# A two-layer gated cross-attention block: the experts of a group issued between the two halves of the attention of the next groups

## What is computed

```python
# layer 0, attention: 16 heads of 16; the last 16 context tokens have weights and a softmax of their own
q = ln(heads(norm(x) @ Wq + bq))
k, v = ln(heads(ctx[:, :48] @ Wk + bk)), heads(ctx[:, :48] @ Wv + bv)
kd, vd = ln(heads(ctx[:, 48:] @ Wkv_dca + bkv_dca))      # v not normalised
x = x + tanh(g_xattn[0]) * ((attn(q, k, v) + attn(q, kd, vd)) @ Wo + bo)
# layer 0, feed-forward: 16 experts of width 64, the best 4 of each token, and one shared expert
w = topk(softmax(norm(x) @ gate_w.T), 4)
y = sum_e w[e] * (silu(h @ Wg[e]) * (h @ Wu[e])) @ Wd[e] + sigmoid(h @ sg) * shared(h)
x = x + tanh(g_ffn[0]) * y
# layer 1: attention with 16 heads of 128 (8 for keys and values), then a SwiGLU of width 688
```

## Time and profile before

| | us |
|---|---|
| median of three runs | 492.94 |
| profiled execution, its own time | 496.02 |
| its span, first to last instruction | 494.2 |
| TensorE matmul busy | 414.4 (84%) |
| VectorE busy | 342.6 (69%) |
| ScalarE busy | 206.3 (42%) |
| GpSimd busy | 161.9 (33%) |

### The profile page before, as it was taken

One profiled execution on the slowest core, in us unless ns is written; L12 is line 12 of the kernel. 1 busy time (PEld: TensorE's weight loads), 2 busy tenths in 40 slices (PEclk: granted clock), 3 DMA queues, 4 the chain that ended last, 5 costly groups with the idle time before them and its releaser, 6 DMA issues. The chain is left out here.

```text
span 494.2 us, 8704 instructions
## 1 busy us (share of the span) xinstructions
PE 414.4 (84%) x2996; PEld 389.1 (79%) x3004; DVE 342.6 (69%) x754; ACT 206.3 (42%) x405; POOL 161.9 (33%) x194
## 2 busy tenths in 40 slices
PE   0647794957666899999999899999999999879996
PEld 0536683847555898999999899999999999869995
DVE  4775749577520666858686398988988988966652
ACT  3264536535222133334334246455555546513331
POOL 3013322142230022222313144464464464334332
PEclk9958596885955699999999899999999999989999
DMA  8103001010110003020020100100100100000000
GB/s 248 43 1 96 32 8 57 0 65 0 28 79 1 0 1 106 0 90 16 19 87 0 58 12 2 55 1 0 55 0 0 44 1 1 1 0 23 23 17 27
DMA packets 6633, 16.03 MB, mean 32 GB/s; under 512 B 1090, under 2 KB 4291, under 8 KB 6100
## 3 DMA queue, kind: packets, MB, share of 16 engines
q1 hardware_dynamic: 6612, 15.75, 9.7%
HBM read 14.70 MB, written 1.05 MB: 32 GB/s over the span
## 5 line engine op out<-in xcount | busy, mean ns | idle before, releaser
L1421 POOL TENSOR_SCALAR work<-work,lut_step,lut 128x344 f32<-128x344 int32 (+1 forms) x60 | 41.7, 709 | 57.4 <-DVE work L1348 55.7
L291 PE MATMUL ps<-wB_hi,workr 128*128 128x256 f32 x224 | 52.0, 295 | 6.0 <-POOL workr L1576 4.6
L291 PE MATMUL ps<-xT_hi,wB_hi 128*128 128x256 f32 x176 | 52.5, 298 | 0.0
L291 PE MATMUL ps<-xT_lo,wB_hi 128*128 128x256 f32 x176 | 50.7, 288 | 0.0
L291 PE MATMUL ps<-xT_hi,wB_lo 128*128 128x256 f32 x176 | 50.7, 288 | 0.0
L291 PE MATMUL ps<-wN_hi,shared_r 128*128 128x256 f32 x256 | 47.8, 281 | 1.3 <-DVE x L1335 1.3
L1014 POOL TENSOR_TENSOR workr<-work,workr 128x256 fp32r<-128x256 f32 (+1 forms) x36 | 23.0, 638 | 69.7 <-ACT workr L897 69.7
L291 PEld LDWEIGHTS ps<-wB_hi,workr 128*128 128x128 f32 x224 | 38.9, 191 | 8.1 <-POOL wB_lo L1426 3.8
L1363 DVE COPY_PREDICATED work<-work 128x1376 f32<-128x1376 int32 (+5 forms) x36 | 42.5, 1182 | 2.7 <-DVE work L1363 0.3
L291 PEld LDWEIGHTS ps<-wN_hi,shared_r 128*128 128x128 f32 x256 | 40.3, 188 | 1.5 <-DVE shared_r L1325 1.5
L291 PE MATMUL ps<-xT_hi,wM_hi 128*128 128x256 f32 x128 | 37.5, 293 | 4.0 <-ACT work L1189 2.4
(11 more groups left out here) (199 smaller groups left out, 1188.9 us busy)
## 6 DMA issues: line engine op xcount, KB each, us to landing
stage<-in_wC SPq DMA_DIRECT2D x4, 1280.0 KB, 5.3
stage<-in_wB SPq DMA_DIRECT2D x4, 768.0 KB, 4.3
stage<-in_idx SPq DMA_DIRECT2D x4, 536.0 KB, 3.4
stage<-in_wA SPq DMA_DIRECT2D x2, 512.0 KB, 5.5
out<-x SPq DMA_DIRECT2D x4, 256.0 KB, 2.2
x<-in_x SPq DMA_DIRECT2D x1, 768.0 KB, 6.9
ctx_T<-in_ctx_T SPq DMA_DIRECT2D x1, 512.0 KB, 7.8
ctx_n<-in_ctx_n SPq DMA_DIRECT2D x4, 128.0 KB, 2.2
```

What stands on the lines that cost most here:

```text
L291: last = nc.tensor.matmul(out, l, r, start=start and i == 0, stop=stop and i == 2)
L1421: nc.gpsimd.tensor_scalar(lev[:, j, 0:n], bits[:, 0, 0:n], lut_step[:, j:j + 1], lut[:, 2 * j:2 * j + 1], ALU.mult, ALU.add).then_inc(*C[" ...
```

## The change

Stages A and B become one sequence of five steps, g = -1 to 3, written out instead of looped: step g holds the experts of group g, the second half of attention of group n = g + 1 and the first half of group m = g + 2, as far as they exist. Step -1 has no experts, step 2 no first half, step 3 the experts alone. C and D stay.

- The banks are dealt anew. B has two gate banks (0 and 1) where it had three, one bank (2) for logits, comb and spread, where spread had two, and one (3) for both tiles of the output. A has banks 4 to 7: the scores of tile 0 in 4 and 5, those of tile 1 in 6 and 7, and everything of the second half (turned probabilities, values, output) in 6 and 7. gate_up(k) waits for h2(k - 2), spread(k) for h3(k - 1), probabilities of tile 1 for the copy of tile 0's.
- All 16 joins move to step 3, two behind each gate_up, over four banks. The weights are loaded in turn into stage and into wC_odd, which lies where A's weights were, and so is loaded once A has ended.
- The four quarters of wB are loaded at the start, ahead of wS and sel on SP's queue, into wB_raw, which lies under wB_lo. They are split in step -1, and TensorE waits for the last of them ahead of step 0.
- Normalising x moves from VectorE to ScalarE, with an offset -mean * rstd made by two further instructions on GpSimd. The copies of the keys' pieces on VectorE (six of eight) move to ScalarE, in three lots: 0, then 1 and 2, then 3. A's turned x has tiles of its own (xTA).
- Where tiles are no longer free by the order of the lists, waits are added (vz for pv_done, ctxm for kv_done, xn for xT_done).

The diff, cut to this (unchanged indentation of eight columns left out):

```diff
+with nc.sbuf_tensor("as_loaded", [P, 2 * NWA + GROUPS * GB], F32) as loaded:
+    wC_odd, wB_raw = loaded[:, 0:GCW], loaded[:, 2 * NWA:2 * NWA + GROUPS * GB]
...
+def front_pool_offset(pool, f):
+    front_pool(pool, f)
+    pool.wait_ge(*front["rstd_ready"].at(f, 1))
+    pool.sem_inc(waited, 1)
+    for t in range(TILES):
+        nc.gpsimd.tensor_scalar(offset[:, t:t + 1], mv[:, t, 0:1], rstd[:, t:t + 1], -1.0, ALU.mult,
+                                ALU.mult).then_inc(*front["offset_ready"].up())
+def front_norm_act(act, f, g):
+    act.wait_ge(*front["offset_ready"].at(f, TILES))
+    if not isinstance(f, int) or f:
+        act.wait_ge(*front["xT_done"].at(f, 0))
+    for t in range(TILES):
+        nc.scalar.activation(xn[:, t, :], x[:, g * TILES + t, :], ACT.Identity, scale=rstd[:, t:t + 1],
+                             bias=offset[:, t:t + 1]).then_inc(*front["xn_ready"].up())
...
+SC = (4, 6)
+KV = (5, 4)
+QK = (4, 5)
+PROBS, VALUES = 6, 6
+A_FRONT, B_FRONT, TURN_OUT, OUT_A = 4, 1, 6, 7
...
+def pe_A_probs(pe, n, t):
+    pe.wait_ge(*A["probs_ready"].at(n, 2 * t + 2))
+    if t == 0:
+        pe.wait_ge(*A["exp_ready"].at(n, TILES))
+    else:
+        pe.wait_ge(*A["pT_ready"].at(n, t))
...
+def pe_A_values(pe, n, t):
+    if t == 0:
+        pe.wait_ge(*A["pT_ready"].at(n, TILES))
+        pe.wait_ge(*A["kv_ready"].at(n, 6))
...
+def act_A_k(act, n, pairs=range(PAIRS0)):
+    act.wait_ge(*A["qT_done"].at(n, 2))
+    for p in pairs:
+        for i, (lo, hi) in enumerate(PARTS):
+            r = slice(32 * p, 32 * p + 32)
+            nc.scalar.activation(kx[r, :, p, lo:hi],
+                                 ps[r, QK[1], :].rearrange("p (k n) -> p k n", n=S)[:, :, lo:hi], ACT.Identity,
+                                 scale=cols[r, 2 + 2 * i:3 + 2 * i], bias=cols[r, 3 + 2 * i:4 + 2 * i]
+                                 ).then_inc(*A["kT_ready"].up())
...
-def dve_A_k(dve, n):
-    dve.wait_ge(*A["qT_done"].at(n, 2))
-    for p in range(PAIRS0 - 1):
-        for i, (lo, hi) in enumerate(PARTS):
-            r = slice(32 * p, 32 * p + 32)
-            nc.vector.tensor_scalar(kx[r, :, p, lo:hi],
-                                    ps[r, 5, :].rearrange("p (k n) -> p k n", n=S)[:, :, lo:hi],
-                                    cols[r, 2 + 2 * i:3 + 2 * i], cols[r, 3 + 2 * i:4 + 2 * i],
-                                    ALU.mult, ALU.add).then_inc(*A["kT_ready"].up())
...
+    if not isinstance(n, int) or n:
+        dve.wait_ge(*A["pv_done"].at(n, 0))
...
+def pe_B_gate_up(pe, g, k):
+    pe.wait_ge(*Bp["h2"].at(g, k - 1))
...
+def pe_B_spread(pe, g, k):
+    if k == 0:
+        pe.wait_ge(*Bp["combT_hi"].at(g, 1))
+        pe.wait_ge(*Bp["combT_lo"].at(g, 1))
+    else:
+        pe.wait_ge(*Bp["h3"].at(g, k))
+    nc.tensor.matmul(spread_to, sel[:, k, :], comb_rows, start=True, stop=True).then_inc(*Bp["bc_done"].up())
...
+def pe_join(pe, j):
+    i, r = j // 4, j % 4
+    wqT, wkT, wvT, wo1 = join_source(i)
+    pe.wait_ge(B_prep_in[i % 2], 16 * (i // 2) + 16)
+    if j >= 4:
+        pe.wait_ge(join_lo, j - 3)
...
+def pe_AB(pe, g, experts, second, first):
+    n, m = g + 1, g + 2
+    last = experts and not second
+    if experts:
+        pe_B_logits(pe, g)
+    if second:
+        pe_A_shift(pe, n, 0)
+        pe_A_shift(pe, n, 1)
+    if experts:
+        pe_B_gate_up(pe, g, 0)
+        pe_B_gate_up(pe, g, 1)
+        if last:
+            pe_join(pe, 0)
+            pe_join(pe, 1)
+    if first:
+        pe.wait_ge(*A["exp_ready"].at(n, 1))
+        pe_A_kv(pe, m, 0)
+    if experts:
+        pe_B_comb(pe, g)
+        pe_B_gate_up(pe, g, 2)
+        if last:
+            pe_join(pe, 2)
+            pe_join(pe, 3)
+    if first:
+        front_pe(pe, front_A(m), A_FRONT)
+    if experts:
+        pe_B_spread(pe, g, 0)
+        pe_B_gate_up(pe, g, 3)
+        if last:
+            pe_join(pe, 4)
+            pe_join(pe, 5)
+    if first:
+        x_split(pe, front_A(m))
+        pe_A_kv(pe, m, 1)
+    if experts:
+        pe_B_spread(pe, g, 1)
+        pe_B_down(pe, g, 0)
+    if second:
+        pe_A_probs(pe, n, 0)
+    if experts:
+        pe_B_gate_up(pe, g, 4)
+        if last:
+            pe_join(pe, 6)
+            pe_join(pe, 7)
+    if first:
+        pe.wait_ge(*A["kv_ready"].at(m, 2))
+        pe_A_q(pe, m)
+    if experts:
+        pe_B_spread(pe, g, 2)
+        pe_B_down(pe, g, 1)
+    if second:
+        pe_A_probs(pe, n, 1)
+    if experts:
+        pe_B_gate_up(pe, g, 5)
+        if last:
+            pe_join(pe, 8)
+            pe_join(pe, 9)
+        pe_B_spread(pe, g, 3)
+        pe_B_down(pe, g, 2)
+    if second:
+        pe_A_values(pe, n, 0)
+        pe_A_values(pe, n, 1)
+    if experts:
+        pe_B_gate_up(pe, g, 6)
+        if last:
+            pe_join(pe, 10)
+            pe_join(pe, 11)
+        pe_B_spread(pe, g, 4)
+        pe_B_down(pe, g, 3)
+    if first:
+        pe_A_turn(pe, m)
+    if second:
+        pe_A_turn_out(pe, n)
+    if experts:
+        pe_B_gate_up(pe, g, 7)
+        if last:
+            pe_join(pe, 12)
+            pe_join(pe, 13)
+        pe_B_spread(pe, g, 5)
+        pe_B_down(pe, g, 4)
+    if second:
+        pe_A_out(pe, n)
+    if experts:
+        pe_B_gate_up(pe, g, 8)
+        if last:
+            pe_join(pe, 14)
+            pe_join(pe, 15)
+        pe_B_spread(pe, g, 6)
+        pe_B_down(pe, g, 5)
+    if first:
+        pe_A_scores(pe, m, 0)
+    if experts:
+        pe_B_spread(pe, g, 7)
+        pe_B_down(pe, g, 6)
+    if first:
+        pe.wait_ge(*A["o_biased"].at(n, 1))
+        pe_A_scores(pe, m, 1)
+    if experts:
+        pe_B_spread(pe, g, 8)
+        pe_B_down(pe, g, 7)
+    front_pe(pe, front_next(g), B_FRONT)
+    if experts:
+        pe_B_down(pe, g, 8)
...
+def act_AB(act, g, experts, second, first):
+    n, m = g + 1, g + 2
+    last = experts and not second
+    def joins(*js):
+        for j in js if last else ():
+            act_join(act, j)
+    if second:
+        act_A_exp(act, n, 0)
+    if experts:
+        act_B_router(act, g)
+        act_B_tanh(act, g, 0)
+    if second:
+        act_A_exp(act, n, 1)
+    if first:
+        front_norm_act(act, front_A(m), m)
+    if experts:
+        act_B_tanh(act, g, 1)
+        joins(0, 1)
+        act_B_comb(act, g)
+        act_B_tanh(act, g, 2)
+    else:
+        act_A_prep(act, 0)
+    joins(2, 3)
+    if first:
+        front_upper(act, front_A(m), A_FRONT, xTA_hi)
+    if experts:
+        act_B_upper(act, g, 0)
+        act_B_tanh(act, g, 3)
+    joins(4, 5)
+    if second:
+        act_A_probs(act, n, 0)
+    if experts:
+        act_B_upper(act, g, 1)
+        act_B_tanh(act, g, 4)
+    else:
+        act_A_prep(act, 1)
+    joins(6, 7)
+    if second:
+        act_A_probs(act, n, 1)
+    if first:
+        act_A_square(act, m)
+        if not experts:
+            act_A_load_ln(act, m)
+    if experts:
+        act_B_upper(act, g, 2)
+        act_B_tanh(act, g, 5)
+        joins(8, 9)
+        act_B_upper(act, g, 3)
+    if first:
+        act_A_guess(act, m)
+    if second:
+        act_A_an(act, n)
+    if experts:
+        act_B_tanh(act, g, 6)
+        joins(10, 11)
+        act_B_upper(act, g, 4)
+    if second:
+        act_A_upper(act, n)
+    if first:
+        act_A_qk(act, m)
+        act_A_k(act, m, (0,))
+    if experts:
+        act_B_tanh(act, g, 7)
+        joins(12, 13)
+        act_B_upper(act, g, 5)
+    if first:
+        act_A_k(act, m, (1, 2))
+    if experts:
+        act_B_tanh(act, g, 8)
+        joins(14, 15)
+        act_B_upper(act, g, 6)
+    if first:
+        act_A_k(act, m, (3,))
+    front_norm_act(act, front_next(g), after(g) if experts else 0)
+    if experts:
+        act_B_upper(act, g, 7)
+    else:
+        act_A_prep(act, 2)
+        act_A_prep(act, 3)
+    front_upper(act, front_next(g), B_FRONT)
+    if experts:
+        act_B_upper(act, g, 8)
+    if first and m + 1 < GROUPS:
+        act_A_ctx(act, m + 1)
...
+def dve_AB(dve, g, experts, second, first):
+    n, m = g + 1, g + 2
+    last = experts and not second
+    def joins(*js):
+        for j in js if last else ():
+            dve_join(dve, j)
+    if experts:
+        dve_B_choose(dve, g)
+        dve_B_gated(dve, g, 0)
+        dve_B_route(dve, g)
+        dve_B_gated(dve, g, 1)
+    joins(0, 1)
+    if second:
+        dve_A_sum(dve, n, 0)
+    if experts:
+        dve_B_comb(dve, g)
+    if first:
+        dve_A_kv(dve, m, 0)
+    if experts:
+        dve_B_gated(dve, g, 2)
+        dve_B_weighted(dve, g, 0)
+    joins(2, 3)
+    if first:
+        front_lower(dve, front_A(m), A_FRONT, xTA_hi, xTA_lo)
+    if second:
+        dve_A_sum(dve, n, 1)
+    if experts:
+        dve_B_gated(dve, g, 3)
+        dve_B_weighted(dve, g, 1)
+    joins(4, 5)
+    if first:
+        dve_A_kv(dve, m, 1)
+    if experts:
+        dve_B_gated(dve, g, 4)
+        dve_B_weighted(dve, g, 2)
+    joins(6, 7)
+    if first:
+        dve_A_q(dve, m)
+    if experts:
```

(86 more changed lines are left out.)

806 lines of the change are left out of this document (333 added, 473 removed).

## The result

The changed kernel takes **518.6 us**, the median of four runs (517.3 to 519.2), where the kernel before takes 493.0 (491.5 to 495.4): the ratio is 1.050, with an interval of 1.046 to 1.055. I had forecast 502, in a range of 480 to 515. So the direction that I gave 0.60 came, and the size is beyond the range.

What follows compares the result with a forecast made beforehand. Attention was taken as a chain with gaps, experts as TensorE-bound. 83.5 + 54 + 54 + 42.5 + 42.6 = 276.6, 3.3 behind the old 273.3; 5.5 for the clock made +9, so 502 us, range 480 to 515.

Steps and rivals of the forecast that it cites:

- I add 1.5 at the first logits, 1.5 for each middle step, 1 for the other two together: 5.5: Allowance for TensorE running at 1.2 GHz behind idle waits in the steps: 5.5 us, between nothing and 16.
- (f): Middle step, before the scores: TensorE waits for all eight key pieces, 3.4 us.
- (d): Middle step, before the turn (pe_A_turn): TensorE waits for VectorE's scale, 3.1 us.
- Rival 3: Waits keep TensorE's clock low as in the attention (0.83): 4.5 us more per middle step, 4 elsewhere, so 515; chance 0.18.
- First logits: Start of the experts' first routing logits, behind the step without experts: forecast at 83.5 us.
- Middle steps: The two steps with experts and both attention halves: 54 us each, 41 of TensorE's work and 13.4 of waits.
- Third step: Step g = 2, no first half of attention: 32 us of work and 10.5 of waits, 42.5.
- Last step: Experts alone with all 16 joins: 38 us of work and 4.6 of tail waits, 42.6.
- The interleaving by itself gives nothing in two of the four steps: Middle steps: 54 us walked against 31.0 + 23.3 = 54.3 replaced, joins apart; old waits filled, new ones of the same length.
- Rival 2: TensorE holds the steps, short ScalarE and VectorE instructions running closer together at (d) and (f): 480 us; chance 0.30.
- Rival 4: The two effects cancel, so the time stays the same, 491.4 to 494.4 us; chance 0.10.
- (c): Middle step, down(2): TensorE waits for h_hi(2), which ScalarE makes after a probs copy and act_A_square, 1.8 us.

Runs made afterwards that it cites:

- e2: Changed kernel with unread identity transposes on TensorE ahead of its long waits (10 to 36 at each of seven places, some semaphore waits added): 500.1 us, ratio 1.013.
- e1: Changed kernel with six of the eight key pieces made on VectorE again, ScalarE keeping one pair: 515.1 us, ratio 1.043.
- e4: Changed kernel with VectorE's scale of q and k right behind the variance, ahead of the values copy: 516.6 us, ratio 1.046.
- e5: Kernel before the change, with identity transposes in front of TensorE's waits in the attention only: 483.6 us, ratio 0.981.
- e10: Changed kernel with half of e2's transposes at each place, e2's added waits kept: 507.3 us, ratio 1.029.
- e3: Changed kernel with the last two quarters of the experts' weights split earlier on ScalarE and GpSimd: 516.2 us, ratio 1.045.
- e11: Changed kernel with only e2's 26 transposes ahead of the scores, the other counts 0, e2's added waits kept: 520.1 us, ratio 1.055.

## Why the prediction was wrong

**The step that failed is "I add 1.5 at the first logits, 1.5 for each middle step, 1 for the other two together: 5.5".** e2 measures this term at 16.6, so it accounts for 11.1 of the 14.2 by which the span was missed (517.2 against 503). The mechanism was right and its size was not. I had a price of 1.6 for a restart, read behind an idle time of 1.53, and ten waits, 16 in all, which stood there only as the upper end. What made 5.5 of it was that "part of what is lost comes out of the next wait", and that was assumed from nothing. Wait (f) shows it best. In e2 TensorE comes to the scores at full clock, spends 3.00 us on 26 transposes and waits 0.72 more, 3.7 in all; in the kernel after, with the lower clock behind wait (d), the wait is 3.68 as well. Nothing was taken back. By the queues the reason is that what TensorE waits for at (d) and (f) is made from its own earlier work, gate_up(6) and the turned output, so the chain is late by the same amount; this is an argument, and no run takes it apart.

That 16 comes so close to 16.6 is partly luck, since single waits don't cost 1.6 each: behind the one of 5.18 the clock is at 0.50 and 0.61 for 8 us, behind those of 3.23 and 3.68 at 0.59 and 0.50 for 4 us, and behind one of 1.62 it stays up here and falls in e1 and e4. Rival 3 took the attention's 0.83 in the earlier trace rows for all the waits, gave 515 and began at the right mechanism; it had 0.18. Its source is partly luck as well, as in the old loop's own turns the low clock cost nearly nothing (e5).

**The rest of the sum.** My sum, clock included, put the end of the experts at 282.1. It came at 296.28 - 1.40 = 294.9, 12.8 later. First logits: I put them 0.6 too late. Middle steps at full clock: 53.9 against 54. Third step: 45.5 in e2 against 42.5, 3.0 missing. Last step: 43.5 in e2 with the wait of 1.40 behind it, 42.1 without, against 42.6. Together -0.6 + 11.1 - 0.2 + 3.0 - 0.5 = 12.8. Behind the experts I had counted nothing, and the third stage took 1.6 more, 220.9 where it took 219.3; in e2 it takes 497.5 - 279.77 = 217.7, so this too goes with the clock. 12.8 and 1.6, less 0.1 for the shorter last wait, are the 14.2 of the span but for rounding. The median was missed by 16.6: I had set it 1 below the span's 503, as the kernel before has it, and it came 1.4 above 517.2.

In the third step the tail is what I walked too short. TensorE's waits there, in the kernel after:

```profile
PE ps L708 <- POOL workr L832: 7.1, 7, 2.4
PE ps L698 <- DVE work L772: 2.6, 1, 2.6
PE ps L698 <- DVE workr L814: 1.1, 1, 1.1
PE ps L688 <- DVE work L810: 1.0, 1, 1.0
```

They sum to 11.8 against my 10.5, and down products come behind GpSimd's lower part seven times. That is 1.3 of the 3.0. In e10, in the same order, the step takes 43.94 at clock 1.00, so some 1.5 of the 3.0 is clock that e2 hadn't won back, and 1.4 is the order.

**"The interleaving by itself gives nothing in two of the four steps".** This compared unlike things: the walk of 54 at full clock against the old 31.0 + 23.3, of which the 31.0 holds a clock of 0.83. As a reading of the rows that was wrong, but e5 shows that it did no harm there: at a clock of 1.00 two middle turns of the old loop still take 59.6, 29.8 each, and 29.8 + 23.3 is 53.1 against 53.9. Where it did harm is the third step, which I let hide 29.9 us of attention. With the clock at 1.00 that part is 21.2 (28.4 without, both from its first shift), 44.5 with the experts, and the step of 45.5 hides next to nothing. With fills in both, the new order costs up to 17.2 more. The direction still came for the sum's own reason: a new order near full clock, against the old one with what it loses to the clock, is 279.77 against 274.87 in the traces, 4.9 slower where I had 3.3. What the sum couldn't show is how dear the order is by itself.

**Rival 2 fell.** (d) and (f) were 3.23 and 3.68 against the walk's 3.1 and 3.4; nothing in these two chains ran closer together than its durations say by an amount that counts. Rival 4 fell with the measurement. Of the signs, the time of the first logits and the two releasers came as said; the middle steps took 60.2 and 58.2 where 52 to 57 was the sign of being right. The scores came 47.1 behind the logits where I had 45, and 45.0 behind them in e2.

**Costs that I took at nothing or bounded.** A single load of the experts' weights took twice the time that I gave it, but the four overlap: issued from 9.5 us on, the last at 10.9, and landing within 11.2 us of its issue, they are all in by about 22, where I had 27. The Ln load of the step without experts starts at 57.19, takes 1.28, and the activation behind it starts at 58.48, so no drain shows there. The Trainium skill (ScalarE: Activation LUTs, What ACT_TABLE_LOAD costs) adds a drain of about 1.38 us to a load; by it, as an estimate, (d) would have been 3.1 + 2.3 = 5.4. It was 3.23, so this trace does not agree with the page. The GpSimd offset pair took 0.50 (0.5 assumed) and the ScalarE norm 1.09 (0.8 assumed). Written-out steps weren't tried apart; the walks leave no room for more than some tenths in a middle step. That ScalarE's key pieces release the scores is as forecast, and e1 shows it by taking that wait away, though most of it came up again at the down products; e4 does it for VectorE's scale, and e3 for GpSimd's split of the weights ahead of the first logits.

## What to carry to other kernels

Walk every in-order queue before you interleave two stages: a walk by durations from the trace was right to 0.2 us in 54. But walk both orders at the same clock, and then price the clock by itself, from windows of this kernel behind waits of the same length, since the 11.7 us of waits in the second middle step cost another 4.3 at the lower clock. Whether the next wait takes a part of it back is to be read too: here it took nothing back in the new order, and nearly all in the turns of the old loop, where a clock of 0.77 to 0.83 brought to 1.00 gained 0.7 in 60. Where a wait can't be removed, transposing the identity into a free bank is cheap (10 to 36 transposes), and it was worth 18.5 us on the changed kernel and 9.4 on the kernel before (493.0 to 483.6), most of it in one step.

## What the runs showed that I hadn't expected

- **Equal gaps, unequal clocks.** Behind wait (c), with TensorE busy 2.38 us of the 4 in both kernels shown, the clock stayed at 1.00 in one and fell to 0.56 and 0.50 in the other. Each is one execution, so whether the kernel or the execution decides this, no run tells. Before the first logits, in code that e11 doesn't touch, the clock was 0.84 in the kernel after and 0.76 in e11, worth 3.3 us. A single wait of this size can't be priced by the total time.
- **Half the fill, half the gain or more.** Half of the transposes gave 11.3 of 18.5, with some 3 us of uncertainty: a shortened wait is worth having, even where the rest of it stays.
- **A wait that is taken away can move.** e1's came up again at the down products and before the first logits, and its trace shows 0.8 us less of waits in a middle step where 3.68 was removed.
- **A low clock that cost nothing.** In the old loop two turns at 0.78 and 0.77 took 60.3 us, and 59.6 with the clock held at 1.00 (e5); in the changed kernel two steps at 0.86 and 0.88 lost 10.6 to it (e2). The granted clock alone doesn't say what it costs.
- **A load took twice its time** where four of them are asked for within 1.85 us: 7.0 to 11.2 us each, median 9.1, against 4.3 for the same 768 KB. All four together were still quicker than four loads of 4.3 one after the other. No run took them apart.
